# One loop body for the gate blocks of a recurrent layer: both operands by DMA, blocks of 104 columns

## The reference, cut

```python
x = x + attention(x, cond)                 # [4, 512, 512]; norm, 16 heads, softmax, projection
def cell(h, x_t):                          # GRU, 512 steps, h is [4, 512]
    gi = x_t @ W_ih + b_ih
    gh = h @ W_hh + b_hh
    r = sigmoid(gi_r + gh_r); z = sigmoid(gi_z + gh_z)
    n = tanh(gi_n + r * gh_n)
    return (1 - z) * n + z * h
x = x + scan(cell, cond, x over time)
x = x + depthwise_causal_conv(x, taps=cond)         # 4 taps
x = x + depthwise_causal_conv(x, taps=cond) + b3
```

## Time and profile before

| | |
|---|---|
| median of 3 runs | 2255.23 us |
| the profiled execution | 2253.05 us, of which the span is 2251.1 us |
| PE busy | 2137.5 us, 95% |
| DVE, ACT, POOL busy | 1396.2, 1179.6, 1136.2 us |
| granted PE clock, mean | 0.99 |
| first start of L1101 | 621.7 us |

### The profile page before, as it was taken

The page is one execution under the profiler, slowest core; times in us unless marked ns, Lnnn a source line. Parts: engine busy times, 40 slices in busy tenths (PEclk is TensorE's granted clock), DMA queues, the critical chain, the costliest instruction groups (busy, mean ns, idle before and its releaser), DMA issues.

```text
span 2251.1 us, 183848 instructions
## 1 busy us (share of the span) xinstructions
PE 2137.5 (95%) x75456; PEld 1602.7 (71%) x75456; DVE 1396.2 (62%) x5052; ACT 1179.6 (52%) x5992; POOL 1136.2 (50%) x3895
## 2 busy tenths in 40 slices
PE   6899999999999999999999999999999999999997
PEld 1222222222399999989999988899999888888886
DVE  1434434444266776777677766777777777777775
ACT  2344444443255555555555555555555565555654
POOL 1142432333145555565555555655555666666665
PEclk8899999999999999999999999999999999999999
DMA  6000000001122221101222110022211000000000
GB/s 243 1 1 1 1 1 1 1 20 57 44 54 59 56 55 45 33 7 37 74 54 58 46 47 5 19 74 58 56 51 46 12 7 24 5 7 5 5 7 19
DMA packets 123332, 78.69 MB, mean 35 GB/s; under 512 B 18496, under 2 KB 119104, under 8 KB 122432
## 3 DMA queue, kind: packets, MB, share of 16 engines
q1 hardware_dynamic: 123056, 74.65, 11.9%
q10 hardware_dynamic: 144, 2.10, 0.2%
HBM read 26.37 MB, written 12.58 MB: 17 GB/s over the span
## 4 chain that ended last, share of the span: by engine, by line
PE 65%; DVE 6%; issue 2%; ACT 0%; POOL 0%; POOLq 0%; DVEq 0%
PE ps L1101 59%; PE ps L1128 5%; DVE arena L942 4%; DVE arena L959 1%; ACT ps L1034 0%; PE ps L1135 0%; POOL arena L1176 0%; ACT arena L1059 0%; DVE arena L992 0%; POOL arena L1180 0%; ACT arena L1065 0%; ACT arena L1070 0%; POOL arena L1182 0%; DVE seq L972 0%; DVE arena L980 0%
## 5 line engine op out<-in xcount | busy, mean ns | idle before, releaser
L1101 PE MATMUL ps<-whh,arena 128*4 128x128 f32 (+1 forms) x65536 | 1458.8, 246 | 56.3 <-DVE arena L959 43.0
L1101 PEld LDWEIGHTS ps<-whh,arena 128*4 128x4 f32 x65536 | 1335.3, 87 | 175.3 <-DVE arena L959 114.4
L1059 ACT ACTIVATE arena<-arena 128x8 f32<-128x8 f32 x1024 | 215.8, 211 | 685.5 <-DVE arena L942 677.4
L942 DVE STREAM_TRANSPOSE arena<-ps 128x128 f32<-128x128 f32 x1024 | 435.6, 425 | 207.4 <-PE ps L1101 203.9
L1176 POOL TENSOR_TENSOR arena<-tap,seq 128x32 f32<-128x32 f32 x1024 | 231.5, 258 | 288.6 <-DVE seq L972 288.6
L381 DVE TENSOR_REDUCE top<-ps 128x2 f32<-128x1024 f32 x128 | 150.7, 1219 | 258.2 <-PE ps L620 258.2
L959 DVE TENSOR_TENSOR_SCAN arena<-arena 128x24 f32<-128x24 f32 x1024 | 214.5, 209 | 145.0 <-ACT arena L1070 145.0
L1034 ACT ACTIVATE ps<-arena 128x128 f32<-128x128 f32 x1026 | 269.6, 263 | 0.3 <-PE ps L1135 0.3
L948 DVE STREAM_TRANSPOSE arena<-ps 128x64 f32<-128x64 f32 x1024 | 255.4, 249 | 19.2 <-PE ps L1101 9.9
L1176 POOL TENSOR_TENSOR arena<-tap,arena 128x32 f32<-128x32 f32 x1024 | 231.5, 257 | 66.8 <-POOL arena L1186 66.8
L523 PE MATMUL ps<-arena 128*32 128x512 f32 x2048 | 247.7, 604 | 11.5 <-POOL arena L214 11.5
(11 more groups left out here) (91 smaller groups left out, 1373.5 us busy)
## 6 DMA issues: line engine op xcount, KB each, us to landing
arena<-arena SPq DMA_DIRECT2D x384, 64.0 KB, 1.9
arena<-seq SPq DMA_DIRECT2D x192, 64.0 KB, 2.0
arena<-gi_d SPq DMA_DIRECT2D x256, 32.0 KB
gi_d<-arena SPq DMA_DIRECT2D x96, 64.0 KB, 1.6
seq<-in_x SPq DMA_DIRECT2D x4, 1024.0 KB, 17.3
whh<-in_w_hh SPq DMA_DIRECT2D x1, 3072.0 KB, 20.1
out<-seq SPq DMA_DIRECT2D x3, 1024.0 KB, 5.4
arena<-in_w_emb ACTq DMA_DIRECT2D x1, 2048.0 KB, 8.8
```

The costliest lines, as they stand in the source:

```text
L942: e.transpose(trn[:, h].rearrange("p q (i c s) -> p q c i s", c=2, s=2)[:, :, :, :, 0], bank[RN[h]][:, 0:P].rearrange("p (q c i) -> p q c ...
L1059: e.activation(r_d0[:, h].rearrange("p (i s) -> p i s", s=2)[:, :, 1], trn[:, h, 0, 0:2 * NH].rearrange("p (i s) -> p i s", s=2)[:, :, 0], ...
L1101: last = e.matmul(bank[dst[h]][32 * G:32 * G + B, 0:n], hv, wv[:, k, gates, G, 64 * h:64 * h + 64], start=False, stop=k2 == 1 and k == C - ...
```

## The change

The blocks get one form. A list `BLOCKS`, built in Python, has 184 of them: for each tile 40 for r and z (4 batches x 10 blocks of 104 columns; the tenth begins at column 920 and overlaps the ninth by 16) and for n 16 blocks for each group of 104 time steps beginning at 128, 232, 336 and 408 (two groups in the first tile, one in each other). They take steps 0 to 367 without a break; steps 368 to 511 are bare. The stationary operand now comes by DMA too, into `fixed`, whenever it differs from that of the block before (12 times for r and z, 16 times for n); the moving operand comes in two transfers for each block in place of four, of 2 x 104 columns for each partition. One semaphore for each half (`s_pair`) counts both, so `part` has one wait where it had two. With both operands at fixed places PE needs one loop over all blocks and one over the bare steps. DVE's steps with blocks are written out, 368 of them, with constants for the counts; its bare steps are one loop. SP's code is straight-line as before.

```diff
+        BW = 104
+        RZ_AT = [min(BW * j, 2 * D - BW) for j in range(-(-2 * D // BW))]
+        N_AT = [P + min(BW * j, T - P - BW) for j in range(-(-(T - P) // BW))]
+        BLOCKS = []
+        for i in range(TB - 1):
+            BLOCKS += [("rz", i + 1, b, first) for b in range(B) for first in RZ_AT]
+            for first in (N_AT[0:2], N_AT[2:3], N_AT[3:4])[i]:
+                BLOCKS += [("n", first, c, b) for c in range(C) for b in range(B)]
...
-        blk = tile([P, 2, P])
-        moving = tile([P, C, P])
+        blk = tile([P, 2, BW])
+        fixed = tile([P, C, P])
+        moving = tile([P, C, BW])
...
-                def bring_moving(q, k):
...
-                    e.dma_start(moving[:, k, :], src).then_inc(s_moving[k], 16)
+                def bring_pair(q, v):
...
+                    if held == held_before:
+                        e.sem_inc(s_pair[v], 16)
+                    else:
+                        e.dma_start(fixed[:, ks, :], weights).then_inc(s_pair[v], 16)
+                    e.dma_start(moving[:, ks, :], src).then_inc(s_pair[v], 16)
...
+                for step in range(2, T, 2):
+                    q = step // 2 - 1
+                    if q < NBLOCKS:
+                        if q + 1 < NBLOCKS:
+                            for v in range(2):
+                                e.wait_ge(st["s_part"], 2 * q + v + 1)
+                                bring_pair(q + 1, v)
+                        keep(q)
+                    if step % HALF == 0 and step + HALF < T:
...
+                        next_half(first)
+                    if step % P == 16 and step > P:
+                        store(e, *stores[step // P - 1])
...
+                for q in range(NBLOCKS):
+                    for v in range(2):
+                        step(2 * q + v, v)
+                    take(q)
+                with e.Fori(NBLOCKS, T // 2) as it:
+                    for v in range(2):
+                        step(it * 2 + v, v)
...
+                def part(v, q):
+                    if v == 0:
                         e.wait_ge(st["s_taken"], e.snap(q + 1))
+                    e.wait_ge(s_pair[v], e.snap(q * 32 + 32))
+                    for k in (2 * v, 2 * v + 1):
                         for g in range(NG):
+                            rows = slice(32 * g, 32 * g + 32)
+                            last = e.matmul(bank[FB][rows, 0:BW], fixed[:, k, rows], moving[:, k, :],
                                             start=k == 0, stop=k == C - 1)
+                    last.then_inc(st["s_part"], 1)
...
+                with e.Fori(0, NBLOCKS) as q:
+                    for v in range(2):
+                        step(q * 2 + v, v)
+                        part(v, q)
+                with e.Fori(NBLOCKS, T // 2) as it:
+                    for v in range(2):
+                        step(it * 2 + v, v)
```

More of the change, by code:

```diff
@@ L840, in tile @@
             return v.rearrange("p (a b c) -> p a b c", a=shape[1], b=shape[2])
+        BW = 104
[6 more added lines that the diff above has]
+                BLOCKS += [("n", first, c, b) for c in range(C) for b in range(B)]
+        NBLOCKS = len(BLOCKS)
+        N_RZ = [sum(x[0] == "rz" for x in BLOCKS[:q]) for q in range(NBLOCKS + 1)]
         NH = NI // 2
@@ L857, in build @@
         s_kept = [sem("s_kept0"), sem("s_kept1")]
-        s_moving = [sem(f"s_moving{k}") for k in range(C)]
+        s_pair = [sem("s_pair0"), sem("s_pair1")]
         RN, RZ, FB = (0, 1), (2, 3), 4
         N_CLEAR = 9
-        TILE_BLOCKS = B * 2 * NG + C * B
         def h_of(u, h):
@@ L897, in _ @@
                     e.sem_inc(s_kept[i], 16)
[L898 to L919, removed]
-                        next_half(first)
-                        first += HALF
@@ L922, in _ @@
[L922 to L926, removed]
+                for v in range(2):
+                    bring_pair(0, v)
+                for step in range(2, T, 2):
[7 more added lines that the diff above has]
+                    if step % HALF == 0 and step + HALF < T:
+                        first = step + HALF
+                        if first % P == 0:
+                            for i in range(2):
+                                e.wait_ge(s_kept[i], 16 * (1 + first // P * B * len(RZ_AT) // 2))
+                        next_half(first)
+                    if step % P == 16 and step > P:
+                        store(e, *stores[step // P - 1])
@@ L935, in step, with count @@
                 def step(t, u):
-                    half = (e.snap(2 * t + 1), e.snap(2 * t + 2))
-                    h4 = e.snap(2 * t + 4)
-                    now = e.snap(t + PAD)
+                    def count(v):
+                        return v if isinstance(v, int) else e.snap(v)
+                    half = (count(2 * t + 1), count(2 * t + 2))
+                    h4 = count(2 * t + 4)
+                    now = count(t + PAD)
                     def turn_rn(h):
@@ L974, in step, with take @@
                                     ALU.add).then_inc(st["s_x3"], 1)
[L976 to L987, removed]
+                def take(q):
+                    kind, a, b, c = BLOCKS[q]
+                    e.wait_ge(st["s_part"], 2 * q + 2)
+                    if kind == "rz":
+                        e.wait_ge(s_kept[N_RZ[q] % 2], 16 * (1 + N_RZ[q] // 2))
+                        e.tensor_tensor(blk[:, N_RZ[q] % 2], bank[FB][:, 0:BW], bias_rz[:, c:c + BW], ALU.add
+                                        ).then_inc(st["s_taken"], 1)
+                    else:
+                        e.tensor_scalar(gate_of(b)[:, c, a:a + BW], bank[FB][:, 0:BW], vecT[:, b, R_BN:R_BN + 1], None,
+                                        ALU.add).then_inc(st["s_taken"], 1)
                 c = st["s_clear"]
```

25 lines of the change are left out of this document (14 added, 11 removed).

## The result

The changed kernel takes 2243.9 us (median of 5, 2241.51 to 2244.54); the kernel before took 2255.23 us beside it (5 runs). The ratio is 0.9944, 95% interval 0.9929 to 0.9959: faster by 11.3 us where 33.7 were forecast, above the middle of the range and close to rival A's 2241.8. The profiled execution took 2244.54 us, its span is 2242.5. One execution of the runs further down is in no ratio: of the four of `e9_late_pe4` one took 3954 us, at a mean granted clock of 0.80 where the others have 0.99, and nothing here explains it.

The account below looks back on a forecast made before the run. Bare steps bound by the circle PE, DVE, ACT, DVE, steps with half a block by PE's queue. 1146.3 + 432.6 + 2 = 1580.9 us against 1614.6, 33.7 less: median 2221.5 us, range 2207 to 2245.

Parts of the forecast that it names:

- rival A: PE's half blocks: narrower width gives nothing, being fixed queue work, and the slips stay; 13.4 us less, 2241.8 us; chance 0.17.
- Item 5: Breaks between PE's loops: 24 + 4 loops become two, 2 us in place of 25.6 + 1.5.
- Bare steps: Steps without blocks: 143 of them at 3.025 us each, 432.6 us.
- Item 1: PE's half blocks, 128 to 104 columns: 0.08 us less each; periods become 3.01 and 3.21 us.
- long period: PE's step in which the loop's branch is taken: 3.23 to 3.21 us; staying at 3.23 would show the forecast wrong.
- short period: PE's step without the loop's branch: 3.07 to 3.01 us, then bound by the circle PE, DVE, ACT, DVE.
- Item 2: DVE's steps with blocks written out, no branch or counts: gain 0.02 us a step, bounds 0 and 0.02.
- Rows 8: Profile rows of DVE in a short step: 0.34 us scan against mean 0.202, read as lateness from the loop's branch.
- Item 6: Block transfers, two of 104 KB in place of four of 64 KB: hidden within 5.9 us, cost 0.
- C: PE's one loop falls into a bad place: 0.07 us a step, 26 us back, 2247.5 us; chance 0.06.
- D: Transfers with 416-byte lines come late, 7.6 us landing: 313 us more, 2534 us; chance 0.04.
- E: DVE's written-out code stalls on fetches, one block in four: 49 us, giving 2270 us; chance 0.05.

Follow-up runs that it names:

- e9_late_pe4: Changed kernel with two semaphore increments ahead of DVE's add to `seq` in written-out steps and PE's block loop four steps long: 2214.1 us, ratio to before 0.9816.
- e3: Changed kernel with blocks of 128 columns in place of 104, 144 blocks over steps 0 to 287: 2227.3 us, ratio to before 0.9867.
- e11: Changed kernel with 128-column blocks and two semaphore increments ahead of DVE's add to `seq` in written-out steps: 2223.9 us, ratio to before 0.9857.
- e8: Changed kernel with two semaphore increments ahead of DVE's add to `seq` in the written-out steps: 2221.0 us, ratio to before 0.9841.
- e12: Changed kernel without POOL's two convolutions, POOL only waiting and counting, so the output isn't the reference's: 2212.7 us, ratio to before 0.9815.
- e10: Changed kernel with two semaphore increments ahead of DVE's add to `seq` and PE's block loop eight steps long: 2866.1 us, ratio to before 1.2697.
- e1: Changed kernel with three more semaphore increments on POOL after its wait for the state, in every pair: 2239.0 us, ratio to before 0.992.

## Why the prediction was wrong, point by point

- **Item 5, breaks: right.** 27.1 us of breaks were to become 2. Idle on "issue" is 1.6 us, no code is fetched for PE while the loop with blocks runs (640 to 1780 us), and with width and number of steps with blocks unchanged the stretches of the recurrence fall from 1614.6 us to 1590.0 with the collision (e3) and to 1586.7 without it (e11).
- **Bare steps: right.** 432.6 us forecast, 432.61 measured.
- **Item 1, width: right in mechanism, a little off in the long period.** The half block streams 0.54 us for 0.63. The circle then sets the short period; without the collision that is 3.01, as forecast (e8). The long period stays at 3.225 to 3.24 us at either width (e8, e11), which the prediction had named as a sign of being wrong: there the width gives its lower bound, 0, and not 0.02. Against the forecast's 3.21 that is 184 x 0.028, some 5 us.
- **Item 2, DVE without loops: the step that failed.** I bounded it by 0 and 0.02 us a step, a gain or nothing, because DVE had no branch and no counts to compute any more. I didn't follow who is released by a faster DVE. The add to `seq` comes 0.1 us earlier, POOL starts earlier, and its addition falls on the scan in the circle. The sum had 0.02 us a step of gain here (3.15 for 3.17); the run shows 0.06 us a step lost: 23.4 us over 368 steps by e8 against the changed kernel, 24.3 by e12. It makes up nearly the whole miss of 1174.5 - 1148.3 = 26.2 us. The other 3 us are the 5 of the long period above and 1.5 of late transfers, less nearly 4 that the sum had for breaks (2 us) and for what it couldn't place (0.005 us a step, 1.8 us).
- **Rows 8, misread.** I took the scan of 0.34 us for a slip of DVE's branch that would go. POOL's addition had begun 0.03 us ahead of it (689.75): it was one case of what the change made the rule.
- **Item 6, transfers: right to 1.5 us.** They land in 2.1 us. The store of a tile took 6.7 us and not 5.4 beside them, over the 5.9 us of cover, and PE waited twice for 0.7 to 0.8 us.
- **Rival A** gave the right number for the wrong reason: the width did take its 0.08 us off the half block. It was right in that the slips stayed, and that the long period didn't follow the width. **C**: PE's 128 matmuls take 2.83 us in the median and over 2.90 in two steps of 512. **D**: no doubling with 416-byte lines; the rule of the Trainium skill, page "DMA: Bandwidth & Descriptors", section "Specifications", on transfers under 512 bytes shows no cost in landings here: 2.1 us for 104 KB in 416-byte lines, and 2.1 to 2.2 for the 128 KB transfers in 512-byte lines of the same run. **E**: no idle of DVE on "issue"; 37 transfers of code on the other queue ran beside the work. By that the rule of the Trainium skill, page "Runtime: NRT & Kernel Launch", section "Instruction fetch mechanics", on code fetched in sequence agrees with the trace for DVE, and e10 agrees with its other half: a branch to code that is no longer held costs a fetch each time.

The late add gave 2221.0 us, against 2221.5 forecast. An agreement within 0.5 us is luck. By the stretches e8 takes 1585.1 us where the forecast had 1580.9, and its profiled execution lies 1.4 us above its median, where the forecast put the median 2.2 above the profiled one. But without the collision the sum held to about 4 us.

## What to carry to other kernels

When an edit makes one engine faster, ask whom it releases, and what that engine's next operation will lie beside; a gain of 0.1 us off the critical path cost 0.13 us on it. An operation that reads longer than its mean in one row is a question to be settled before it is used, by looking at what the other engines do in the same 0.3 us. Merging loops removed 25 to 28 us of first passes at once (e3, e11). Narrowing the blocks to spread them over more steps was worth nothing (e8 against e11): the short period fell by 0.07 us, but 80 more steps carried a block, and every second one of them then took the 3.24 us of the long period, where a bare one takes at most 3.05.

## What the runs showed of the hardware that I had not expected

- A DVE scan of 128x16 f32 takes 0.192 us in the median and at most 0.194 with POOL idle (1024 scans of e12), and up to 0.36 us when it starts while a POOL tensor operation on SBUF is under way: it then ends 0.047 us after the end of the POOL operation (3958 of 3969 such scans within 6 ns). When the scan starts first it keeps its 0.19 us. For the addition the two cases part at 5 to 6 ns between the starts, and an order decided by 0.02 to 0.03 us is worth 23 us of the kernel.
- A loop of PE is free of fetches at two and four steps long and not at eight: 2221, 2214 and 2866 us, everything else alike.
- In bare steps POOL has so little room that 0.24 us more in each pair makes it the bound: 6.05 us for two steps become 6.26 (e1). In the changed kernel 0.117 us pass on its queue up to the end of the wait for DVE, and 0.096 in e1, where DVE is long done (medians): a room of 0.02 us.
